# A graph network's edge sums: PE's main loop as an engine loop over four units, in place of 100 unrolled units

## What is computed

```python
def _max_cut_grad(x, src, dst, edge_weight, num_nodes):
    msg = x[src] * edge_weight[:, None]
    return jax.ops.segment_sum(msg, dst, num_segments=num_nodes)

def lift_step(h, wb):
    W, b = wb
    g = _l2_normalize(_max_cut_grad(h, src, dst, edge_weight, N))
    out = jnp.concatenate([h, g], axis=1) @ W + b
    return (_l2_normalize(out), None)
```

## Time and profile before

| | |
|---|---|
| median of 3 runs | 12909.68 us (12894.7 to 12926.64) |
| profiled execution, own time | 12883.4 us |
| its span in the trace | 12881.8 us |
| PE busy / DVE busy | 62% / 73% of the span |
| chain that ended last | PE 29%, DVE 21%, issue 16% |
| granted TensorE clock, mean | 0.765 |

### The profile page before, as it was taken

One profiled execution on the slowest core, in us unless ns is written; L12 is line 12 of the kernel. 1 busy time (PEld: TensorE's weight loads), 2 busy tenths in 40 slices (PEclk: granted clock), 3 DMA queues, 4 the chain that ended last, 5 costly groups with the idle time before them and its releaser, 6 DMA issues.

```text
span 12881.8 us, 342702 instructions
## 1 busy us (share of the span) xinstructions
PE 7922.8 (62%) x130026; PEld 5298.1 (41%) x130039; DVE 9363.2 (73%) x19419; ACT 3162.7 (25%) x7975; POOL 4996.6 (39%) x5027
## 2 busy tenths in 40 slices
PE   2444444410376777776776777777667777777773
PEld 1333333300365666665665666666522222222221
DVE  7666666637665675666666666666699999999995
ACT  0000000008421212212211212212134444444431
POOL 2666666620112112111111111111077777777771
PEclk9999999995678787787787787787755565555555
DMA  4000000017645454454454454454422212222221
GB/s 152 21 21 21 21 20 21 21 69 285 203 136 149 134 153 136 132 168 120 132 166 119 135 161 132 139 161 135 116 43 36 35 35 35 35 35 35 35 34 17
DMA packets 717799, 1210.29 MB, mean 94 GB/s; under 512 B 176136, under 2 KB 338731, under 8 KB 713491
## 3 DMA queue, kind: packets, MB, share of 16 engines
q1 hardware_dynamic: 433940, 1057.96, 25.5%
q0 software_dynamic: 146832, 68.64, 5.9%
q10 hardware_dynamic: 136012, 67.95, 2.1%
HBM read 1051.25 MB, written 140.48 MB: 93 GB/s over the span
## 4 chain that ended last, share of the span: by engine, by line
PE 29%; DVE 21%; issue 16%; another core or an unknown queue 7%; DMA 3%; POOL 2%; DVEq 1%; ACT 1%; SPq 0%; POOLq 0%; ACTq 0%
PE psum L1927 10%; PE psum L1959 8%; PE psum L1942 6%; DVE space L1439 3%; DVE space L1472 2%; DVE space L1473 2%; PE psum L2034 2%; DMA space<-src_rows 2%; DVE space L1435 2%; DVE space L1407 1%; PE psum L2004 1%; DVE space L1417 1%; DVE space L1484 1%; DVE space L1477 1%
## 5 line engine op out<-in xcount | busy, mean ns | idle before, releaser
L787 POOL DMA_INDIRECT space<-feature_table,space x2000 | 2422.1, 1211 | 615.2 <-issue 614.9
L714 POOL TENSOR_TENSOR claim_out<-claim_in 128x1 f32<-128x1 f32 x443 | 94.8, 214 | 6431.4 <-DMA table<-space 2772.0
L1138 DVE TENSOR_TENSOR space<-psum,space 128x320 f32<-128x320 f32 x2400 | 1065.8, 485 | 1769.1 <-PE psum L1942 1740.1
L1622 ACT ACTIVATE space<-psum 128x375 f32<-128x375 f32 x2400 | 952.4, 435 | 3886.4 <-PE psum L1927 2877.6
L2050 PE MATMUL psum<-w_mix,space 64*128 64x448 f32 x4144 | 1842.3, 986 | 0.0
L1959 PE MATMUL psum<-space 128*128 128x96 bf16 x24000 | 1472.1, 214 | 472.3 <-issue 410.8
L723 POOL DMA_INDIRECT slots<-space x1568 | 1510.5, 963 | 449.3 <-issue 413.8
L1927 PE MATMUL psum<-space 128*32 128x125 fp8e4 x72000 | 1483.7, 230 | 310.0 <-issue 304.1
L1959 PEld LDWEIGHTS psum<-space 128*128 128x128 fp8e4 x24000 | 1199.3, 101 | 716.8 <-issue 608.4
L1927 PEld LDWEIGHTS psum<-space 128*32 128x32 bf16 x72000 | 1165.2, 101 | 619.7 <-issue 613.1
L1942 PE MATMUL psum<-identity,space 128*128 128x128 f32 x6000 | 964.7, 296 | 359.5 <-ACT space L1622 346.6
(11 more groups left out here) (278 smaller groups left out, 12198.9 us busy)
## 6 DMA issues: line engine op xcount, KB each, us to landing
space<-marks SPq DMA_DIRECT2D x2400, 320.0 KB
space<-src_rows SPq DMA_DIRECT2D x102, 640.0 KB, 4.7
marks<-space SPq DMA_DIRECT2D x100, 640.0 KB, 3.1
space<-distances ACTq DMA_DIRECT2D x200, 320.0 KB
space<-block_ids SPq DMA_DIRECT2D x198, 200.0 KB
slots<-space SPq DMA_DIRECT2D x82, 448.0 KB, 9.2
space<-feature_table,space POOLq DMA_INDIRECT x2072
slots<-space POOLq DMA_INDIRECT x1608, 2.1
```

The lines of the kernel that those rows point to most:

```text
L787: g.indirect_dma_start(out=gathered_rows[0:SLOTS, half, t, :], out_offset=None, in_=feature_table, in_offset=bass.IndirectOffsetOnAxis(ap= ...
L1138: v.tensor_tensor(row[:, half, :], slots_of_unit[:, half, :], slot_w[:, bass.ds(at * UNIT_TILES + k * HALF_TILES, HALF_TILES)].rearrange(" ...
L1622: a.activation(to[:, s0:s1, :, :], pair_picked[:, bank, 0:(s1 - s0) * PICK_COLS].rearrange("p (k c r) -> p k c r", k=s1 - s0, r=CAP), ACT.Copy
```

## The change

PE's code for a layer becomes loops of the engine: a body of four units (`four_units`), run once to open a chunk, then four times in a loop, in a loop over the first four chunks; the last chunk stands apart, since it ends without a gather for a next unit. With constant addresses in the body, what changes from unit to unit must lie in few places: the ring of marks gets four places (`RING = 4`), and the source parts, which were read from `parts` at the unit's own address, are copied by ACT (`spread_parts`, 480 bf16 elements per partition) into one of two places of `part_ring`, one unit ahead of the gather. At a layer's start PE waits for ACT's first copy (`parts_spread`) in place of `parts_ready`. After each inner loop the last unit of a chunk is added apart (`end_chunk`), with one small extra matmul ahead of it.

```diff
-    RING = 5
+    RING, PART_RING = 4, 2
...
                     a.activation(hg[:, :, 0:D], h, ACT.Copy).then_inc(h_copied, 1)
+
+                    def spread_parts(q):
+                        return a.activation(part_ring[:, q % PART_RING, :, :, :].rearrange("p s c d -> p (s c d)"),
+                                            parts[:, q * SRC_PER_TILE:(q + 1) * SRC_PER_TILE, :, :].rearrange(
+                                                "p s c d -> p (s c d)"), ACT.Copy)
+
+                    act.wait_ge(parts_ready, layer + 1)
+                    spread_parts(0).then_inc(parts_spread, 1)
                     with act.Fori(0, CHUNKS, 1) as j:
                         for q in range(STEPS):
+                            spread_parts((q + 1) % STEPS)
                             n = layer * UNITS + j * STEPS + q
...
-                                          parts[:, q * SRC_PER_TILE + s, c, :], cells[:, :, g, CAP * s:CAP * (s + 1)],
+                                          part_ring[:, q % PART_RING, s, c, :], cells[:, :, g, CAP * s:CAP * (s + 1)],
...
-            def add_chunk(layer, j, more):
-                first = (layer * CHUNKS + j) * STEPS
-                for q in range(STEPS):
-                    if q + 1 < STEPS or more:
-                        await_picks(layer, j + (q + 1) // STEPS, (q + 1) % STEPS)
-                    turn_slots(first + q, q)
-                    if q + 1 < STEPS:
-                        gather(layer, first + q + 1, q + 1)
-                    elif more:
-                        gather(layer, first + STEPS, 0)
-                    if q == 1:
-                        clear_unit_sums(layer * CHUNKS + j)
-                    if q:
-                        add_unit(layer, j, first + q - 1, q - 1)
-                add_unit(layer, j, first + STEPS - 1, STEPS - 1)
+            def four_units(first, opens=None, closes=False):
+                loads, twice = pe.snap(first * (16 // RING)), pe.snap(first * 2)
+                for k in range(RING):
+                    if not (closes and k + 1 == RING):
+                        await_picks(loads + 16 * ((k + 1) // RING + 1), k + 1)
+                    turn_slots(twice + (2 * k + 2), k)
+                    if not (closes and k + 1 == RING):
+                        gather(k + 1)
+                    if opens is None or k >= 1:
+                        if opens is not None and k == 1:
+                            clear_unit_sums(opens)
+                        if k:
+                            add_unit(loads + 16, twice + 2 * k, k - 1)
+                        else:
+                            add_unit(loads, twice, RING - 1)
+
+            def end_chunk(first, after_loop):
+                loads, twice = pe.snap(first * (16 // RING)), pe.snap(first * 2)
+                add_unit(loads + 16, twice + 2 * RING, RING - 1, after_loop)
 
             with pe.Fori(0, LAYERS, 1) as layer:
-                pe.wait_ge(parts_ready, layer + 1)
-                await_picks(layer, 0, 0)
+                pe.wait_ge(parts_spread, layer + 1)
+                await_picks(layer * (16 * UNITS // RING) + 16, 0)
                 mm(slots_of_unit[:, 0, :], zeros_bf[:, 0:LANES], zeros_bf[:, 0:D], start=True, stop=True)
-                gather(layer, layer * UNITS, 0)
-                for j in range(CHUNKS):
-                    add_chunk(layer, j, j + 1 < CHUNKS)
+                gather(0)
+                with pe.Fori(0, CHUNKS - 1, 1) as j:
+                    at = pe.snap(layer * UNITS + j * STEPS)
+                    four_units(at, opens=layer * CHUNKS + j)
+                    with pe.Fori(1, STEPS // RING, 1) as m:
+                        four_units(pe.snap(at + m * RING))
+                    end_chunk(at + (STEPS - RING), True)
+                at = pe.snap(layer * UNITS + (CHUNKS - 1) * STEPS)
+                four_units(at, opens=layer * CHUNKS + (CHUNKS - 1))
+                with pe.Fori(1, STEPS // RING - 1, 1) as m:
+                    four_units(pe.snap(at + m * RING))
+                four_units(pe.snap(at + (STEPS - RING)), closes=True)
+                end_chunk(at + (STEPS - RING), False)
```

More of the change, by code:

```diff
@@ L317, in build_gnn @@
         parts = parts_words.bitcast(BF16).rearrange("p (b c d) -> p b c d", c=PARTS, d=D)
+        part_words = carve(2 * UNIT_COLS // 4)
+        part_ring = part_words[:, 0:PART_RING * SRC_PER_TILE * PARTS * D // 2].bitcast(BF16).rearrange(
+            "p (r s c d) -> p r s c d", r=PART_RING, s=SRC_PER_TILE, c=PARTS)
         ring_words = carve(RING, 2 * UNIT_COLS // 4).bitcast(I32)
@@ L486, in build_gnn @@
         parts_ready = sem("parts_ready")
+        parts_spread = sem("parts_spread")
         picks_loaded = [sem(f"picks_loaded{i}") for i in range(RING)]
@@ L1919, in _, with gather @@
             pe.wait_ge(params_loaded, 16 * (6 + 6))
-            def gather(layer, n, q):
+            def gather(q):
                 cells = mark_ring[:, q % RING, 0, :].rearrange("p (c g l) -> p c g l", g=LANE_GROUPS, l=LANES)
@@ L1927, in gather, with await_picks, turn_slots @@
                                 last = mm(pair_picked[D * g:D * (g + 1), bank, (s - s0) * PICK_COLS:(s - s0 + 1) * PICK_COLS],
-                                          parts[:, q * SRC_PER_TILE + s, c, :], cells[:, :, g, CAP * s:CAP * (s + 1)],
+                                          part_ring[:, q % PART_RING, s, c, :], cells[:, :, g, CAP * s:CAP * (s + 1)],
                                           start=c == 0, stop=c == PARTS - 1)
                     last.then_inc(pair_gathered, 1)
-            def loads_of(layer, j, q):
-                return (layer * CHUNKS + j) * (STEPS // RING) + q // RING + 1
-            def await_picks(layer, j, q):
-                pe.wait_ge(picks_loaded[q % RING], 16 * loads_of(layer, j, q))
-            def turn_slots(n, q):
-                pe.wait_ge(pair_copied, 2 * n + 2)
-                pe.wait_ge(weighed, 2 * n + 2)
+            def await_picks(loads, q):
+                pe.wait_ge(picks_loaded[q % RING], loads)
+            def turn_slots(copied, q):
+                pe.wait_ge(pair_copied, copied)
+                pe.wait_ge(weighed, copied)
                 for c in range(COLS_OF):
@@ L1951, in clear_unit_sums, with add_unit @@
                        zeros_bf[:, 0:SUMS_PER_BANK * PARTS * D], start=True, stop=True)
-            def add_unit(layer, j, n, q):
-                pe.wait_ge(bf_ready, 2)
-                pe.wait_ge(places_loaded[q % RING], 16 * loads_of(layer, j, q))
-                pe.wait_ge(least_split, 2 * n + 2)
+            def add_unit(loads, split, q, after_loop=False):
+                if not after_loop:
+                    pe.wait_ge(bf_ready, 2)
+                pe.wait_ge(places_loaded[q % RING], loads)
+                pe.wait_ge(least_split, split)
+                if after_loop:
+                    mm(psum[:, 7 * BANK:7 * BANK + 8], zeros_bf[:, 0:LANES], zeros_bf[:, 0:8], start=True, stop=True)
                 for t in range(UNIT_TILES):
```

## The result

The changed kernel takes 13,080.47 us (median of 4 runs, 13,069.79 to 13,104.23), the kernel before 12,914.63 (4 runs, 12,894.70 to 12,926.64): 1.29% slower, ratio 1.0129 [1.0111, 1.0148]. Forecast were 13,235 and "slower"; the range held. The loss is 166 us where 325 were forecast.

What follows compares the result with a forecast made beforehand. PE and DVE were taken as full at 2.50 us a unit, with fetch stalls and a crawl during POOL's batches on top. 12,883.4 + 294 (ring) + 8 (copies) + 35 (overhead) = 13,220, stated as 13,235; 8-in-10 range 12,700 to 13,750.

Steps and rivals of the forecast that it cites:

- The loop's code stays: PE's main loop: looped code stays resident, fetch stalls go, undisturbed units fall from 2.85 to 2.50 us; best case 294 us.
- The crawl stays: Units with a POOL batch of spill gathers, nine a layer, stay at 13.06 us and those behind them at 4.53.
- Rival 1: The crawl goes too: batch units and those behind fall to 3.20 us, 1,209 us less, 12,020; chance 0.15.
- The ring makes PE wait for marks: Four places make PE wait ahead of its transposes: 70 undisturbed units a layer go from 2.85 to 3.20 us, +294 us.
- The equation: Two unit periods equal issue, marks load, PE's notice, then transposes, gather and adds: 2P = 0.18 + L + 0.1 + 2.71.
- L: Time of a marks load into a ring place: taken as 3.4 us, between 2.2 and 4.7.
- P: Period of an undisturbed unit in the main loop: forecast 3.20 us, bounds 2.60 to 3.85.
- loop overhead: Branches and registers in PE's sequencer cost nothing where PE waits; fetching new code in each layer, 35 us in all.
- The copies are hidden: ACT's part copies, about 0.6 us each, cost nothing except at each layer's start, about 0.7 x 12 = 8 us.
- Rival 3: The four-unit loop body is fetched again each turn, 3 us net, some 23 turns a layer: +830 us, 14,060; chance 0.09.
- Rival 4: The code loop changes nothing, only the ring counts: small stalls stay on top of P, about 13,400; with the forecast, 0.68.

Runs made afterwards that it cites:

- the first comparison: Changed kernel against the kernel before, in the first measurement: 13,080.47 us against 12,914.63, ratio 1.0129.
- the second job: Changed kernel unedited, timed again beside the kernel before, at the high level: 13,025.49 us against 12,866.22, ratio 1.0123; two edited kernels were also timed there.
- the kernel with the ring alone: Kernel before with the marks ring cut from five places to four, code still unrolled: 11,909.51 us against 11,457.79, ratio 1.0398.
- early picks: Changed kernel with the picks half of a place reloaded once its unit is turned: 11,071.12 us, ratio 0.9666 to the kernel before; repeated, 0.9680.
- wait behind the transposes: Changed kernel with PE's wait for unit n's picks put behind the transposes of unit n-1: 12,779.92 us, ratio 0.9926 to the kernel before.
- the longer loop with ring five and copies: Changed kernel with ring of five and a loop body of twenty units, a whole chunk: 12,964.34 us, ratio 1.0068 to the kernel before.
- the first job: Low-level job, kernel before at 11,457.79 us; timed ring of four alone, picks reloaded earlier, one spill gather a unit, and plain transfers for gathers.
- stand-ins: Changed kernel with one spill gather a unit, 11,428.61 us (ratio 0.9972), or plain transfers in place of spill gathers, 11,429.58 and 11,434.53 us; low level.

## Why the prediction was right, step by step

- **The loop's code stays, and takes the fetch stalls with it: shown.** q8 259 where some 250 were said, 13 blocks a layer. What this is worth alone is known only within bounds. Stops by "issue" fell from 0.23 to 0.02 us a unit, 0.21 x 70 x 12 = 176 us, in the first comparison; between two kernels of four places at the low level lie 481 us, which holds the spreading of the gathers too. I had 294, from undisturbed units that would fall from 2.85 to 2.50.
- **The crawl stays: shown.** Batch units of 12.43 us with code that isn't fetched. Rival 1 is out as a mechanism: resident code crawls as unrolled code did. That its units might shorten a little I had at nothing; they gave back 9 x (0.46 + 0.21) = 6 us a layer, 72 in all (in the second job 9 x (0.22 + 0.20) x 12 = 45). When the wait was moved and the other units were quick, batch units took 12.65 again. That part of the crawl falls into time that the ring loses anyway is one reading of it; it was not tested, and cause and size stay open.
- **The ring makes PE wait for marks, two periods to a load: shown**, by the chain above, by the kernel with the ring alone (+452 us) and by the two that take the wait away in different ways (early picks, most units at 2.51 us; wait behind the transposes, 2.71 on the mean). The equation held: with the loads' median of 3.1 it gives (0.17 + 3.1 + 0.24 + 2.70) / 2 = 3.11. But **its term L was mis-sized**: 3.4 us with 0.1 for PE's notice, where the chain has 2.83 and 2.94 with 0.24. So P came to 3.11, not 3.20, and the term is 70 x 0.28 x 12 = 235 us, not 294. The 3.4 had been picked between 2.2 and 4.7, so some of this nearness is luck.
- **The sum was nearly twice too high**: 325 us of loss, of which 166 came. By the traces of the first comparison the terms are 235 for the undisturbed units in place of 294, -72 for batch units and those behind them in place of 0, 20 at chunk ends and first units where I had 35 for loop overhead, and 12 at the layers' starts in place of 8. That makes 195 us in the two traced executions, of which that of the changed kernel is the slowest of its four; the 42 us more ahead of layer 0 and 15 us less behind layer 11 are in none of the terms.
- **The copies are hidden: shown.** 0.60 us each, as said. PE waits for one only at a layer's start, 1.0 us more where 0.7 was said; the longer loop with ring five and copies has undisturbed units no slower than the kernel before.
- **Rival 3, the code doesn't stay**, is what the loop of twenty units does. By the Trainium skill ("Runtime: NRT & Kernel Launch", section on instruction fetch) a branch out of a window of two pages of 256 instructions is a stall; the same section gives TensorE room for 2,048 instructions, 8 blocks. The traces agree with the second figure and not with the first: a chunk's 5.3 blocks stay, 13 don't, and what lies between was not tried.
- **Rival 4** (small stalls stay on top of P) is out: undisturbed units keep 0.02 us of "issue" each. The kernel with the ring alone shows what the rival describes: 0.19 us of "issue" each, and units of 3.51 us.

Open is what the high level is. No trace tells it; the same chip showed the low level in the first job and the high one in the fourth. What is shown: a good part of the excess hangs on POOL's indirect gathers being in a burst (spreading them takes 748 us, 6%, off the kernel before, where some 1,430 us lie between the levels), and at that level PE stops while POOL gathers. Whether the indirect form is needed for it was asked twice and fell on the low level both times. At the low level the change is worth close to nothing: an estimate, since the changed kernel there is known only through its stand-ins (0.997 to 0.999).

## What to carry to other kernels

- When a ring loses a place, write the cycle from "place free" over issue, load and wait to the next "place free", and count how many units it spans; the period follows from it, here to 3% with a guessed load time. Then look at what the cycle contains that need not be in it: a half of the buffer that is free earlier, or work in front of the wait that doesn't read the data. The first gave 3.1% over the changed kernel's stand-ins at the low level, the second 1.9% over the changed kernel at the high one, for a few lines each.
- An engine loop pays when its body and what it turns round in stay resident; watch the instruction queue's blocks per pass. A loop that was too long was worse than straight code here, by some 4 to 5 us at each turn that showed.
- Bursts of POOL's gathers are worth spreading: 0.9% at the low level (on the kernel with early picks), 5.9% at the high one (on the kernel before).

## What the runs showed of the hardware that was not expected

- One program, two levels: 11,442 to 11,458 and 12,866 to 12,915 us for the kernel before, steady within a job. Between the changed kernel at the high level and its stand-in with plain transfers at the low one lie 1,581 us; 1,099 of them lie in the main loops. Before the first layer, where POOL scatters almost without a pause, some 450 us more are spent at the high level: the first transposes of layer 0 start at 3,396.5 us in the changed kernel there, and at 2,945.1 in its stand-in.
- At the high level a gather on POOL stops PE (0.46 us in the middle of 60 queued matmuls, while no code is brought in) and eight in a row hold a unit for 12 to 13 us; at the low level the same instruction, 0.96 us long on both, leaves the sixty matmuls in one piece, and eight in a row cost about 1 us in all.
- PE's loop of 5.3 blocks of code is fetched once a layer (13 blocks); one of 13 blocks is fetched anew each turn (71 a layer), with a stop of up to 4.6 us at the turn.
